# Halved inner position blocks in disentangled attention, and one weight product in linear attention

## The reference

```
x = x + attn_a(layernorm(x));  x = x + ffn(layernorm(x))
x = x + attn_b(layernorm(x));  x = x + ffn(layernorm(x))

attn_a (linear attention, 8 heads of 16):
  q = x @ Wq;  feat = elu(q) + 1;  KV = feat^T (q/L);  msg = feat KV / (feat . sum feat) * L
  msg = msg @ Wm                              # (.., 128) @ (128, 128)
  x = x + layernorm(msg);  x + layernorm(relu(msg @ W1) @ W2)      # W1 (128, 256)

attn_b (disentangled attention, 16 heads of 8, S = 256):
  scores[s,k] = q_s.k_k * c + q_s.pos_k[bucket(s-k)] * c2 + k_k.pos_q[bucket(s-k)] * c2
  ctx = softmax(scores) @ v;  out = ctx @ Wo + bo
```

## Time and profile before

| | |
|---|---|
| median of 3 runs | 1332.01 us (1331.94 to 1335.55) |
| the profiled execution | 1336.09 us, span 1334.2 us |
| granted TensorE clock, mean | 0.891 of full |
| TensorE busy | 1062.7 us (80%) |
| VectorE busy | 953.9 us (71%) |
| ScalarE busy | 683.2 us (51%) |
| GpSimd busy | 563.3 us (42%) |
| linear attention | from about 26 to 110 us |
| attend, with its first fills | from about 402 to 1120 us |

### The profile page before, as it was taken

The page is one execution under the profiler, slowest core; times in us unless marked ns, Lnnn a source line. Parts: engine busy times, 40 slices in busy tenths (PEclk is TensorE's granted clock), DMA queues, the critical chain, the costliest instruction groups (busy, mean ns, idle before and its releaser), DMA issues. The chain is left out here.

```text
span 1334.2 us, 31677 instructions
## 1 busy us (share of the span) xinstructions
PE 1062.7 (80%) x9281; PEld 889.5 (67%) x9281; DVE 953.9 (71%) x3013; ACT 683.2 (51%) x1705; POOL 563.3 (42%) x502
## 2 busy tenths in 40 slices
PE   3992615886544999999999999999999998724786
PEld 2992504775323788888878887888888886624776
DVE  7886664565652978888888888888888885653564
ACT  2346302443362666666666666666666664212343
POOL 2504123764000745455545544454545553005764
PEclk9996556999575999999999999999999998656998
DMA  6930053433088575666756574747566540033331
GB/s 139 200 71 1 1 194 94 121 90 88 24 312 190 125 164 142 154 157 146 160 134 165 133 177 119 175 132 169 141 153 154 146 113 1 1 146 95 115 95 42
DMA packets 75274, 166.01 MB, mean 124 GB/s; under 512 B 8249, under 2 KB 54784, under 8 KB 66528
## 3 DMA queue, kind: packets, MB, share of 16 engines
q1 hardware_dynamic: 69600, 152.81, 45.9%
q0 software_dynamic: 5632, 12.70, 2.7%
HBM read 130.78 MB, written 35.74 MB: 125 GB/s over the span
## 5 line engine op out<-in xcount | busy, mean ns | idle before, releaser
L1196 POOL TENSOR_SCALAR ds_scores<-ds_scores,ds_max 128x256 f32<-128x256 f32 x256 | 346.3, 1353 | 332.1 <-DVE ds_max L1415 332.0
L1407 DVE TENSOR_TENSOR ds_p2c<-ds_bank,ds_p2c 128x512 f32<-128x512 f32 x256 | 175.2, 685 | 80.3 <-PE ds_bank L1245 79.7
L1415 DVE CUSTOM_DVE_ANT_0 ds_scores<-ds_bank,ds_p2c 128x256 f32<-128x256 f32 x512 | 195.8, 419 | 0.6 <-issue 0.3
L1356 ACT ACTIVATE all_xt<-ds_bank 128x512 f32<-128x512 f32 x256 | 154.2, 602 | 75.2 <-PE ds_bank L1263 72.7
L1245 PE MATMUL ds_bank<-all_constants,ds_c2p_t 128*128 128x128 f32 x1024 | 159.0, 278 | 0.0
L1263 PE MATMUL ds_bank<-all_constants,ds_scores 128*128 128x128 f32 x1024 | 154.5, 273 | 1.8 <-ACT all_xt L1356 0.8
L1245 PEld LDWEIGHTS ds_bank<-all_constants,ds_c2p_t 128*128 128x128 f32 x1024 | 116.2, 140 | 35.8 <-issue 24.3
L1263 PEld LDWEIGHTS ds_bank<-all_constants,ds_scores 128*128 128x128 f32 x1024 | 119.9, 140 | 6.8 <-issue 2.2
L1236 PE MATMUL ds_bank<-ds_qr,ds_tab 64*128 64x128 f32 x1024 | 76.2, 289 | 36.5 <-DVE ds_qr L1391 32.4
L1338 ACT ACTIVATE ds_c2p_t<-ds_bank 128x256 f32<-128x256 f32 x256 | 77.8, 399 | 47.2 <-PE ds_bank L1236 47.2
L1252 PE MATMUL ds_bank<-ds_ks,ds_qs 72*128 72x256 bf16 x512 | 98.3, 273 | 1.0 <-DVE ds_max L1415 1.0
(11 more groups left out here) (280 smaller groups left out, 2167.9 us busy)
## 6 DMA issues: line engine op xcount, KB each, us to landing
ds_qr<-scratch_qk SPq DMA_DIRECT2D x32, 1024.0 KB, 10.5
ds_kr<-scratch_qk SPq DMA_DIRECT2D x32, 1024.0 KB, 13.8
ds_tab<-scratch_tables SPq DMA_DIRECT2D x64, 248.0 KB, 10.1
slots_in<-all_zero SPq DMA_DIRECT2D x2, 5180.0 KB, 42.3
ds_qs<-scratch_q_parts SPq DMA_DIRECT2D x32, 288.0 KB
ds_ks<-scratch_k_parts SPq DMA_DIRECT2D x32, 288.0 KB
0fe_xb<-slots_in SPq DMA_DIRECT2D x40, 129.5 KB, 2.2
1fe_xb<-slots_in SPq DMA_DIRECT2D x40, 129.5 KB, 2.2
```

The costliest lines, as they stand in the source:

```text
L1196: pool.tensor_scalar(S[b % NS][:, 1, :], S[b % NS][:, 1, :], mx[:, 2 * b + 1:2 * b + 2], None, ALU.subtract).then_inc(s_sub1, 1)
L1356: act.activation(PT[b], pt2[:, :].rearrange("p (k s) -> p k s", k=2), ACT.Exp).then_inc(s_exp, 1)
L1407: dve.tensor_tensor(z, pt1[b % 2][:, :].rearrange("p (a k) -> p a k", a=2), z, ALU.add).then_inc(s_z, 1)
L1415: last = dve.tensor_tensor_reduce(out=S[b % NS][:, st, :], in0=pqk[b % 2][:, st * SEQ:(st + 1) * SEQ], in1=PC[half][:, st, b, :], scale=1. ...
```

## The change

In linear attention the product Wm1 = Wm times W1 is made once (a transpose of Wm, a copy on ScalarE, a product of 256 columns after the first step's work, a second copy), and h = relu's input comes straight from msgT. L664 and its copy L674 go. TensorE reads its moving or stationary columns from `XT` itself, so the copies into `xt` go (L722), and the hardware loop is written out as 14 steps.

In `attend` the two pair fills of each kind stay, and move to steps 0 to 3. The inner fill of a kind becomes a "near" fill of one bank (half of each side's 128 rows of output, from TAB, as two column tiles of 64: 8 products of 128 rows, 64 stationary and 128 moving columns) and an "edge" fill of one bank (the other halves, which are constant, from ENDS: two bf16 products of 64 stationary and 512 moving columns, as two column tiles). Each of the new banks is copied in two pieces of 64 partitions and 512 elements. The 12 fills are: four pairs in steps 0 to 3, near in step 4, near and far in step 5, edge and far in step 6, far, edge and far in step 7; the banks stay 16.

KS is loaded by three DMAs of 24 rows in place of one, and the mask multiply of KR moves from after step 1 to after step 0. The first transposes of a unit wait for 13 banks.

```diff
 linear_attention, tensor:
-                    pe.wait_ge(s_m2c, n - 1)
+                    pe.wait_ge(s_mtc, n - 1)
+                    pe.wait_ge(s_wmc, 2)
+                    wait_over(pe, s_relu, n - 2)
                     for c in range(2):
-                        last = pe.matmul(ph[:, c * SEQ:(c + 1) * SEQ], W1[:, c * P:(c + 1) * P], m2T[:, :], start=True, stop=True)
+                        last = pe.matmul(ph[:, c * SEQ:(c + 1) * SEQ], Wm1[:, c * P:(c + 1) * P], msgT[:, :], start=True, stop=True)
...
-                if 1 in stages:
-                    pe.wait_ge(s_mtc, n)
-                    pe.matmul(pm2t[:, 0:SEQ], Wm[:, :], msgT[:, :], start=True, stop=True).then_inc(s_m2t, 1)
+                if n == 0:
+                    pe.wait_ge(s_wmc, 1)
+                    pe.matmul(pwm[:, P:P + 2 * D], WmT[:, :], W1[:, :], start=True, stop=True).then_inc(s_wm1, 1)
 attend:
-        RUNS = (((0, 0, 4), (1, 8, 4)), ((0, 4, 4), (1, 12, 4)), ((0, 8, 4), (1, 4, 4)))
-        FILLS = [("near", kind, runs) for kind in range(2) for runs in RUNS] + \
-                [("far", kind, (0, QUADS - 1)) for kind in range(2)] + [("far", kind, (1, 0)) for kind in range(2)]
-        FILLS = FILLS[:6] + [FILLS[6], FILLS[8], FILLS[7], FILLS[9]]
+        INNER = ((0, 8, 4), (1, 4, 4))
+        PAIRS = [[("pair", kind, grp) for grp in (0, 4)] for kind in range(2)]
+        NEAR, EDGE = ([(what, kind, None) for kind in range(2)] for what in ("near", "edge"))
+        FARS = [[("far", kind, where) for where in ((0, QUADS - 1), (1, 0))] for kind in range(2)]
+        FILLS = [PAIRS[0][0], PAIRS[0][1], PAIRS[1][0], PAIRS[1][1], NEAR[0], NEAR[1],
+                 FARS[0][0], EDGE[0], FARS[0][1], FARS[1][0], EDGE[1], FARS[1][1]]
...
-        CONTENT_FILLS = FIRST[8]
+        CONTENT_FILLS = FIRST[FILLS.index(FARS[0][1])] + 1
-        SHARE = [1, 1, 1, 1, 1, 1, 2, 2]
+        SHARE = [1, 1, 1, 1, 1, 2, 2, 3]
 load_parts:
-                sp.dma_start(KS[half][:, :], views["k_parts"][:, rows, cols]).then_inc(s_stack[half], 16)
+                for i in range(3):
+                    sp.dma_start(KS[half][i * 3 * DB:(i + 1) * 3 * DB, :], views["k_parts"][rows, cols]).then_inc(s_stack[half], 16)
 fill, tensor:
+                if what == "edge":
+                    pe.wait_ge(s_stack[half], 16 * 6 * (head + 1))
+                    for side, grp, _ in INNER:
+                        own = slice(side * 64, (side + 1) * 64)
+                        last = pe.matmul(pb[FIRST[n] % 2][own, :], ENDS[half][:, kind, side * FAR + own.start:side * FAR + own.stop],
+                                         (QS, KS)[kind][half][:, :].rearrange("p (b s) -> p b s", b=HALF)[:, :, grp * 16:grp * 16 + 64],
+                                         start=True, stop=True)
+                    last.then_inc(s_bm, 1)
+                    return
+                if what == "near":
+                    for a in range(4):
+                        for side, grp, _ in INNER:
+                            own = slice((1 - side) * 64, (2 - side) * 64)
+                            c = TABLE - SEQ + P * side - 16 * (grp + a) + own.start
+                            last = pe.matmul(pb[FIRST[n] % 2][own, a * P:(a + 1) * P], TAB[half][:, kind, c:c + 64],
                                              mov[:, :].rearrange("p (b g s) -> p g b s", b=HALF, s=16)[:, grp + a, :, :], start=True, stop=True)
+                    last.then_inc(s_bm, 1)
                     return
 copy, scalar:
+                if what in ("near", "edge"):
+                    act.wait_ge(s_bm, done + 1)
+                    for side, grp, count in INNER:
+                        part = side if what == "edge" else 1 - side
+                        own = slice(part * 64, (part + 1) * 64)
+                        dst, of = to[own, side, :, grp * 16:grp * 16 + 64], pb[FIRST[n] % 2][own, :]
...
+                        last = act.activation(dst, of, ACT.Copy)
+                    last.then_inc(s_be, 1)
 heads, vector:
-                        if b == 1 and half == 0 and not (isinstance(head, int) and head == 0):
+                        if b == 0 and half == 0 and not (isinstance(head, int) and head == 0):
                             mask(head, 1, KR, s_kr)
-                        if b == 1 and half == 1 and not last:
+                        if b == 0 and half == 1 and not last:
                             mask(head + 1, 0, KR, s_kr)
```

More of the change, by code:

```diff
@@ L596, in over_steps @@
             step(1, (0, 1))
-            with engine.Fori(2, BATCH - 1) as n:
+            for n in range(2, BATCH):
                 step(n, (0, 1, 2))
-            step(BATCH - 1, (0, 1, 2))
             step(BATCH, (1, 2))
@@ L720, in step @@
                 if 0 in stages:
-                    if not (isinstance(n, int) and n == BATCH - 1):
-                        dve.tensor_copy(xt[:, :], XT[:, bass.ds(n * SEQ + SEQ, SEQ)]).then_inc(s_xt, 1)
                     dve.wait_ge(s_kv, n + 1)
@@ L1221, in fill @@
                     return
-                if where[1][1] != where[0][1] + 8:
-                    for r, (side, grp, _) in enumerate(where):
-                        for a in range(4):
-                            c = TABLE - SEQ + P * side - 16 * (grp + a)
-                            last = pe.matmul(pb[r][:, a * P:(a + 1) * P], TAB[half][:, kind, c:c + P],
+                if what == "edge":
+                    pe.wait_ge(s_stack[half], 16 * 6 * (head + 1))
+                    for side, grp, _ in INNER:
[11 more added lines that the diff above has]
+                            last = pe.matmul(pb[FIRST[n] % 2][own, a * P:(a + 1) * P], TAB[half][:, kind, c:c + 64],
                                              mov[:, :].rearrange("p (b g s) -> p g b s", b=HALF, s=16)[:, grp + a, :, :], start=True, stop=True)
-                        last.then_inc(s_bm, 1)
+                    last.then_inc(s_bm, 1)
                     return
-                side, grp, _ = where[0]
                 for a in range(4):
-                    c = TABLE - SEQ + P * side - 16 * (grp + a)
+                    c = TABLE - SEQ - 16 * (where + a)
                     for tile in range(2):
                         rows = slice(tile * 64, (tile + 1) * 64)
-                        own = mov[rows, :].rearrange("p (b q g h s) -> p h q g b s", b=HALF, q=2, h=2, s=8)[:, 1 - tile, :, grp + a, :, :]
+                        own = mov[rows, :].rearrange("p (b q g h s) -> p h q g b s", b=HALF, q=2, h=2, s=8)[:, 1 - tile, :, where + a, :, :]
                         last = pe.matmul(pb[tile][:, :].rearrange("p (r a n) -> p r a n", r=2, a=4)[:, :, a, :], TAB[half][rows, kind, c:c + P],
@@ L1326, in copy @@
                     return
-                if where[1][1] != where[0][1] + 8:
-                    for r, (side, grp, count) in enumerate(where):
-                        act.wait_ge(s_bm, done + r + 1)
-                        dst = to[:, side, :, :].rearrange("p b (g s) -> p g b s", s=16)[:, grp:grp + count, :, :]
-                        act.activation(dst, pb[r][:, :].rearrange("p (g b s) -> p g b s", g=count, b=HALF), ACT.Copy).then_inc(s_be, 1)
+                if what in ("near", "edge"):
[4 more added lines that the diff above has]
+                        dst, of = to[own, side, :, grp * 16:grp * 16 + 64], pb[FIRST[n] % 2][own, :]
+                        if what == "edge":
+                            of = of.rearrange("p (b s) -> p b s", b=HALF)
+                        else:
+                            dst, of = dst.rearrange("p b (g s) -> p g b s", s=16), of.rearrange("p (g b s) -> p g b s", g=count, b=HALF)
+                        last = act.activation(dst, of, ACT.Copy)
+                    last.then_inc(s_be, 1)
                     return
@@ L1334, in copy @@
                     act.wait_ge(s_bm, done + tile + 1)
-                    at = 0
-                    for side, grp, count in where:
-                        dst = to[:, side, :, :].rearrange("p b (g h s) -> p h g b s", h=2, s=8)[:, 1 - tile, grp:grp + count, :, :]
-                        last = act.activation(dst, pb[tile][:, at * 64:(at + count) * 64].rearrange("p (g b s) -> p g b s", g=count, b=HALF), ACT.Copy)
-                        at += count
+                    for side in range(2):
+                        dst = to[:, side, :, :].rearrange("p b (g h s) -> p h g b s", h=2, s=8)[:, 1 - tile, where + 8 * side:where + 8 * side + 4, :, :]
+                        last = act.activation(dst, pb[tile][:, side * 256:(side + 1) * 256].rearrange("p (g b s) -> p g b s", g=4, b=HALF), ACT.Copy)
                     last.then_inc(s_be, 1)
```

43 lines of the change are left out of this document (20 added, 23 removed).

## The result

The changed kernel took 1341.81 us (median of 7 runs, 1339.81 to 1346.6) against 1332.01 us, a ratio of 1.008 with a 95% interval of 1.0049 to 1.0112. It is slower by 0.5 to 1.1%; the forecast was no change. The profiled execution has a span of 1339.8 us at a granted clock of 0.890.

What follows compares the result with a forecast made beforehand. TensorE bounded attention's 21.51 us unit; ScalarE's copy chain would make it 21.70. Units +5.9, first fills -1.0, linear attention -4.7 gave +0.2 us: 1332 us, no change, range 1316 to 1347 (forecast's own 1323 to 1342).

Steps and rivals of the forecast that it cites:

- Copies on ScalarE: Attention: each 64-partition, 512-element piece takes 0.49 us; four new edge pieces add 2.0 us of ScalarE work per unit.
- Linear attention: Its 13 steps each lose 0.15 us, with 1.3, 0.6 and 0.8 us more at end and start: -4.7 us.
- The loop's fetches cost: Rival: instruction fetches of the written-out loop leave linear attention without gain, +5 us, 1337 us; chance 0.10.
- Near and edge on TensorE: Attention: column tiles run side by side, so a near fill takes 1.09 us and an edge fill's products 0.22 us.
- The rival without overlap: Attention: column tiles of 64 run in turn, near takes 1.88 us, unit 23.3 us, +49 us, 1381 us; chance 0.07.
- ScalarE's tail: Attention steps 5 to 7: ScalarE's copies and exponentials take 4.88 us against TensorE's 4.04, which waits 0.84 us per unit.
- The rival that ScalarE's slack hides it: Attention: cheaper pieces or waits falling in slack make a unit 20.9 to 21.3 us, total 1306 to 1325; chance 0.20.
- Masks and loads at nothing: Attention: KR's earlier mask and the three KS loads stay hidden in the unit and cost 0 us.
- The rival's rule: Attention: KR's mask has 0.5 us to spare; VectorE 1 us later costs 0.5 per unit, +15, 1347 us; chance 0.13.
- First fills: Attention's first fills at the lower clock: cheaper near fills against added edge fills, -1 us, bounds -3 and +2.
- The base: The sum starts from the profiled execution's 1336.1 us, 4.1 us above the runs' median of 1332.0.

Runs made afterwards that it cites:

- the gaps: GpSimd waits for each of its 64 residual additions before the next: in the changed kernel 1336.66 us (ratio 1.0015), in the kernel before 1334.61 us (1.0007).

## Why the prediction was wrong

**Two terms of the sum were mis-sized; the mechanism of the first was right.** The forecast was +5.9 for the units, -1.0 for the first fills, -4.7 for linear attention, no change in all. The measured 1341.8 us is 9.8 over before. It still lies within the stated 1316 to 1347, at the upper edge of the forecast's own 1323 to 1342; but it is told apart from before. By the prediction's own chances no change (0.30) was the least likely of the three outcomes, slower (0.36) the likeliest.

- *Copies on ScalarE: the failed term is "so I take 0.49".* A 64-partition piece behind an operation that starts at another partition came after 0.60 to 0.62 us. The nine operations between the last near product and the last far product hold three such changes (near's second piece, edge's second piece, the far copy behind it). From the near copy's start to the last far product the prediction has 3.92 + 0.60 + 0.06 = 4.58 us; measured 4.90 (714.12 to 719.02). With all pieces on the same partitions the pitch was the 0.48 that I had assumed and the unit 21.5 us, so the pitch is worth 0.39 us a unit, 12 us in all. The other terms of the unit were together 0.19 too dear (near's shorter products are 0.11 of it, and 0.48 where I took 0.49, over the chain, 0.07: 4.51 instead of 4.58), which hid half of the error: 21.70 forecast, 21.91 measured, 6.5 us over 31 units. No bound of mine held it: I had looked for a price under 0.49 and put none above.
- *Linear attention: the failed term is "-4.7 us", which has nothing for GpSimd.* Its own parts were together too cautious: 0.27 a step instead of 0.15, at the end 1.1 instead of 1.3, and with the gaps the changed layer hands over 8.0 us earlier than the layer of before with them. But VectorE stood for 4.20 and 3.04 us beside GpSimd's additions, and the next stage began 1.5 us later. This is 6.2 us off the forecast. No rival had it. "The loop's fetches cost" foresaw a layer that gains nothing, for another reason. The longest durations in the trace of before would not have shown it, since there the same line never took over 0.31 us.
- *Near and edge on TensorE* were right: side by side, 1.02 and 0.41. The rival without overlap falls.
- *ScalarE's tail* was the right place. The idle times of its two products, 0.23 and 0.57 us, sum to 0.80 against the forecast 0.84. The rival that ScalarE's slack hides it falls; its total was reached once the copies were spread, 1311 us, inside its 1306 to 1325, with a unit of 20.81 just under its 20.9.
- *Masks and loads at nothing* was right for this change, with 0.66 us from the mask's end to its reader, less the 0.13 that a hand-over takes (716.55 + 2.29 to 718.97), where I had 0.5. The rival's rule held: it priced a mask 1 us later at 0.5 us a unit, 15 us. A whole step makes it some 1.7 us later, and the 1.1 to 1.2 over the slack cost 36 us.
- *First fills* gained 2.2 us (46.2 to 44.0 between the same two events) instead of 1, inside the bounds.
- *The base.* The sum started from 1336.1 and the forecast from 1332. The two long units of that execution, 3.5 us over the rest, are most of the difference, and the two other traces with both the attention and the loads of before (linear attention alone, and the gaps) don't have them. They hide as much of the difference between the profiled executions, 5.6 us where the medians have 9.8.

## What to carry to other kernels

When an engine has slack on average, write down its operations between two hand-overs one by one, and give each that follows on other partitions its own price. When work leaves the bounding engine for a second one, spread it anew over the steps before judging the change: here the same instructions gave 1.008 in one order and 0.982 in another. When a layer runs beside GpSimd, look in the trace of the changed kernel at the longest duration of each small VectorE operation, not at the median.

## What the runs showed of the hardware

- ScalarE's operations of 512 elements on PSUM followed each other every 0.48 us if both start at partition 0, whether they have 64 or 128 partitions, and after 0.60 to 0.62 us if one starts at 0 and the other at 64, about the time that one takes alone. This held in both directions. Two in a row that start at 64 were not seen.
- VectorE stood in one 128x8 operation for 2.6 to 5.1 us (four times in two traces) beside an unbroken run of GpSimd additions, one every 0.41 us, and ended 0.02 to 0.04 us after a GpSimd operation with a gap behind it. A semaphore wait between the additions removed it. Why the layer of before, with the same operations and additions, never met it was not settled.
- Two tiles of 64 columns by 128 rows run side by side: sixteen instructions of 128 columns in 1.02 us, against 1.88 at the full width. So do two of 64 by 72: two bf16 products of 512 columns in 0.41 us.
- Three transfers of 96 KB in place of one of 288 KB brought the landing of the qr load queued behind them from 10.5 to 7.6 us after its own issue, and of kr from 13.6 to 11.8 (in the kernel before 10.5 to 7.7, and 13.8 to 11.6).
